# A transformer block on one core: the division of the attention output moves from VectorE to GpSimd, with a new order of steps

## The reference

```python
h = layernorm(x) * (1 + ca) + sa
q, k = [content, rotary] parts of 16 heads;  v from the 64-wide latent
attn = softmax(q @ k.T * SCALE + causal_mask)
out  = attn @ v                      # divided by the sums of the exponentials
x = x + ga * (out @ w_out.T)
h = layernorm(x) * (1 + cb) + sb
x = x + gb * mixture_of_8_experts(h) # gate, up, SiLU, weights of the top 8, down
```

## Time and profile before

| | us |
|---|---|
| median of three runs | 1096.62 |
| lowest, highest | 1093.07, 1107.65 |
| the profiled execution, timed | 1096.97 |
| its span in the profile | 1095.0 |
| busy: TensorE, VectorE, GpSimd, ScalarE | 1026.2, 771.5, 412.7, 401.1 |
| mean granted TensorE clock | 0.979 of full |

### The profile page before, as it was taken

One profiled execution on the slowest core, in us unless ns is written; L12 is line 12 of the kernel. 1 busy time (PEld: TensorE's weight loads), 2 busy tenths in 40 slices (PEclk: granted clock), 3 DMA queues, 4 the chain that ended last, 5 costly groups with the idle time before them and its releaser, 6 DMA issues.

```text
span 1095.0 us, 24777 instructions
## 1 busy us (share of the span) xinstructions
PE 1026.2 (94%) x9744; PEld 730.9 (67%) x9744; DVE 771.5 (70%) x1516; ACT 401.1 (37%) x723; POOL 412.7 (38%) x349
## 2 busy tenths in 40 slices
PE   6979989999999989999899999999999998999778
PEld 4646667766677667766677666776677666776456
DVE  5767687585957868677885859678686777857344
ACT  3334533254314443145332543144431453314310
POOL 1526442264505353154422644054441544226100
PEclk9989999999999999999999999999999999999979
DMA  6220000200002000200002000020002000010000
GB/s 191 58 88 2 2 1 1 68 2 2 1 4 67 2 1 1 69 2 2 1 1 69 2 2 1 2 69 2 1 1 69 2 2 1 1 49 2 1 1 20
DMA packets 22232, 23.59 MB, mean 22 GB/s; under 512 B 6314, under 2 KB 20138, under 8 KB 22130
## 3 DMA queue, kind: packets, MB, share of 16 engines
q1 hardware_dynamic: 22130, 22.02, 6.6%
HBM read 17.80 MB, written 4.21 MB: 20 GB/s over the span
## 4 chain that ended last, share of the span: by engine, by line
PE 82%; DVE 11%; issue 4%; ACT 2%; POOL 1%; DMA 1%; POOLq 0%; DVEq 0%; SPq 0%; ACTq 0%
PE ring L1131 17%; PE ring L981 12%; PE ring L982 10%; PE ring L983 10%; PE ring L1203 8%; PE av L1147 7%; PE ring L1107 6%; PE ring L1098 3%; DVE mcol L863 2%; DVE xr L902 1%; PE ring L1115 1%; PE ring L1192 1%; DVE prod L839 1%; PE av L1160 1%; PE ring L1042 1%
## 5 line engine op out<-in xcount | busy, mean ns | idle before, releaser
L672 ACT ACTIVATE pt<-ring 128x384 f32<-128x384 f32 (+1 forms) x384 | 170.9, 532 | 326.2 <-PE ring L1131 289.7
L562 POOL TENSOR_SCALAR_AFFINE_SELECT pt<-pt 128x512 f32<-128x512 f32 x128 | 79.4, 635 | 409.6 <-ACT pt L672 409.6
L863 DVE TENSOR_REDUCE mcol<-ring 128x1 f32<-128x128 f32 (+3 forms) x512 | 212.3, 483 | 19.3 <-PE ring L1107 18.1
L839 DVE TENSOR_TENSOR prod<-ring,table 128x1024 f32<-128x1024 f32 x128 | 155.4, 1219 | 93.1 <-PE ring L983 92.5
L1131 PE MATMUL ring<-rows 32*128 32x512 f32 (+3 forms) x3072 | 175.9, 330 | 9.4 <-ACT pt L672 4.9
L1131 PEld LDWEIGHTS ring<-rows 32*128 32x128 f32 x3072 | 130.4, 184 | 60.6 <-issue 35.0
L553 POOL TENSOR_TENSOR rows<-prod,rows 128x1024 fp32r<-128x1024 f32 x64 | 152.5, 2393 | 36.3 <-ACT rows L652 36.3
L546 POOL TENSOR_TENSOR prod<-prod 128x512 f32<-128x512 f32 x64 | 82.5, 1290 | 134.3 <-DVE prod L839 133.7
L652 ACT ACTIVATE rows<-prod 128x1024 fp32r<-128x1024 f32 x64 | 67.0, 1060 | 60.2 <-PE ring L1131 39.3
L1147 PE MATMUL av<-pt,vals 128*17 128x512 f32 (+3 forms) x1024 | 85.3, 439 | 3.2 <-POOL pt L562 3.2
L1131 PE MATMUL ring<-cont 32*128 32x512 f32 (+3 forms) x1024 | 85.6, 319 | 0.0
(11 more groups left out here) (162 smaller groups left out, 1624.4 us busy)
## 6 DMA issues: line engine op xcount, KB each, us to landing
xn<-x_dram SPq DMA_DIRECT2D x8, 512.0 KB, 4.1
xr<-x_dram SPq DMA_DIRECT2D x8, 512.0 KB, 4.2
out_dram<-xr SPq DMA_DIRECT2D x8, 512.0 KB, 3.2
gate_bc<-gates_scratch SPq DMA_DIRECT2D x8, 256.0 KB, 4.3
pt<-wmod_dram SPq DMA_DIRECT2D x1, 1536.0 KB, 6.6
pt<-gup_t_dram SPq DMA_DIRECT2D x16, 96.0 KB, 2.6
dn<-wu_t_dram SPq DMA_DIRECT2D x1, 640.0 KB, 10.1
xr<-wk_t_dram SPq DMA_DIRECT2D x1, 512.0 KB, 8.3
```

Of the source, the lines that this page charges most:

```text
L672: sc.activation(pt[:, PT_AT[n] + h * w:PT_AT[n] + (h + 1) * w], ps[:, 0:w], ACT.Exp, scale=SCALE).then_inc(exp_ready.sem, 1)
L839: ve.tensor_tensor(prod[:, s % PROD, :, :], ps[:, :].unsqueeze(1).broadcast_to([P, 2, S]), table[:, :, :], ALU.mult).then_inc(rotated.sem, 1)
L863: last = ve.reduce_max(mcol[:, q, h * HR + HD:h * HR + HD + 1], ps[:, at:at + (q + 1) * P], AX_X)
```

## The change

- A step `norm.0 g` on GpSimd does the multiplication of L883 by the inverted sums, the same tiles and shape. It waits for `sums_inverted` of its group, and for even g for `pair_ready` of the pair before, whose data its output overwrites.
- `attn_out` on VectorE keeps the wait for `normalised` of the group before, the turning of `av` and the reciprocal. Its wait for `pair_ready` goes.
- A step `pair.0 i` on VectorE waits for `normalised` of group 2i + 1 and turns the pair.
- BODY_ORDER and LAST_ORDER are new as a whole; SETUP_ORDER stays. The set of the other steps is the same in both.

Read by engine, the part of the new BODY_ORDER around the last group is: on TensorE score.032, rope.1010, qcon.10, value.031, value.032, latent.1, rope.1011, mix.00, mix.01, values.10, kcon.10, rope.1100, qcon.11, rope.1101, rope.1110, turn2.00, turn2.01, maxima.100, rope.1111, logits.0. On VectorE attn_out.02, rotate.1001, rotate.1010, pair.00, attn_out.03, qcon_lo.10, pair.01, latent_lo.1, rotate.1011, mixed, stats2.0, rotate.1100, norm2.0, kcon_lo.10, rotate.1101, qcon_lo.11, rotate.1110, low2. On GpSimd clear.030, combine.100, clear.031, norm.02, clear.032, norm.03, lo.100, combine.101, pow2.0.

```diff
 BODY_ORDER = """
-load_next.1 loads.0 maxima.010 rope.0200 reduce.010 score.000 rotate.0200 rope.0201 exp.000 rotate.0201 maxima.011
-rope.0210 clear.000 reduce.011 score.001 rope.0211 exp.001 rotate.0210 combine.020 clear.001 maxima.012 rotate.0211
-combine.021 value.000 value.001 reduce.012 score.002 hi.020 shift.01 qcon.02 lo.020 exp.002 kcon.02 qcon_hi.02
-clear.002 rope.0300 shifted.01 stats1.1 hi.021 qcon_lo.02 kcon_hi.02 score.010 rotate.0300 pow1.1 value.002 exp.010
-rope.0301 kcon_lo.02 score.011 attn_out.00 lo.021 rope.0310 rotate.0301 exp.011 maxima.020 clear.010 value.010
-rotate.0310 combine.030 reduce.020 score.012 exp.012 norm1.1 rope.0311 maxima.021 qcon.03 rotate.0311 reduce.021
-maxima.022 combine.031 clear.011 qcon_hi.03 kcon.03 hi.030 clear.012 qcon_lo.03 lo.030 hi.031 turn1.10 reduce.022
-value.011 turn1.11 kcon_hi.03 modulate1.10 shift.02 kcon_lo.03 shifted.02 lo.031 maxima.030 reduce.030 value.012
-modulate1.11 low1.10 score.020 exp.020 score.021 low1.11 clear.020 exp.021 attn_out.01 clear.021 rope.1000
-maxima.031 rotate.1000 value.020 reduce.031 maxima.032 reduce.032 value.021 score.022 exp.022 shift.03 shifted.03
-rope.1001 score.030 clear.022 value.022 rotate.1001 exp.030 attn_out.02 latent.1 latent_hi.1 latent_lo.1 combine.100
-score.031 clear.030 value.030 exp.031 score.032 clear.031 rope.1010 exp.032 clear.032 rope.1011 value.031 value.032
-hi.100 lo.100 rotate.1010 rotate.1011 kcon.10 kcon_hi.10 attn_out.03 values.10 rope.1100 combine.101 hi.101 mix.00
-mix.01 values.11 rotate.1100 kcon_lo.10 qcon.10 mixed.00 mixed.01 values_out.10 qcon_hi.10 lo.101 qcon_lo.10
-maxima.100 stats2.0 reduce.100 values_out.11 maxima.101 rope.1101 rope.1110 pow2.0 norm2.0 turn2.00 reduce.101
-turn2.01 rotate.1101 modulate2.00 rope.1111 modulate2.01 qcon.11 qcon_hi.11 rotate.1110 combine.110 low2.00
-maxima.102 low2.01 logits.0 rotate.1111 logits_copy.0 qcon_lo.11 gate.00 hi.110 combine.111 turn_l.0 lo.110
-reduce.102 turned_l.0 tanh.00 hi.111 gate.01 tanh.01 gate.02 tanh.02 gated.00 up.00 up.01 top.0 shift.10 gate.03
-gated.01 gated.02 up.02 ex.0 tanh.03 upped.00 top2.0 gate.04 turn_w.0 wT.0 gated.03 upped.01 up.03 gate.05
-shifted.10 wT_lo.0 upped.02 weigh.00 weigh.01 up.04 tanh.04 upped.03 gated.04 weigh.02 tanh.05 gated.05 weighed.00
-kcon.11 lo.111 up.05 weighed.01 upped.04 weighed.02 weigh.03 weigh.04 weigh.05 upped.05 weighed.03 weighed.04
-kcon_hi.11 weighed.05 down.00 kcon_lo.11 down.01 join.00 join.01 store.0
+load_next.1 loads.0 maxima.010 reduce.010 score.000 exp.000 rope.0200 rotate.0200 maxima.011 clear.000 reduce.011
+rope.0201 score.001 rope.0210 rotate.0201 exp.001 maxima.012 clear.001 rotate.0210 reduce.012 combine.020 value.000
+score.002 rope.0211 shift.01 kcon.02 rotate.0211 exp.002 qcon.02 hi.020 shifted.01 qcon_hi.02 value.001 clear.002
+value.002 combine.021 stats1.1 kcon_hi.02 score.010 hi.021 lo.020 kcon_lo.02 lo.021 rope.0300 qcon_lo.02 attn_out.00
+exp.010 maxima.020 rotate.0300 rope.0301 reduce.020 score.011 rope.0310 rotate.0301 exp.011 maxima.021 rotate.0310
+pow1.1 clear.010 reduce.021 norm.00 norm1.1 value.010 clear.011 score.012 combine.030 rope.0311 rotate.0311 exp.012
+combine.031 hi.030 maxima.022 kcon.03 qcon.03 clear.012 kcon_hi.03 reduce.022 turn1.10 qcon_hi.03 kcon_lo.03
+turn1.11 qcon_lo.03 value.011 hi.031 lo.030 modulate1.10 shift.02 shifted.02 maxima.030 reduce.030 modulate1.11
+value.012 low1.10 low1.11 score.020 exp.020 score.021 exp.021 clear.020 clear.021 attn_out.01 maxima.031 value.020
+reduce.031 norm.01 lo.031 maxima.032 value.021 reduce.032 score.022 exp.022 shift.03 rope.1000 shifted.03 score.030
+rotate.1000 clear.022 value.022 rope.1001 attn_out.02 exp.030 clear.030 rotate.1001 score.031 exp.031 combine.100
+clear.031 value.030 score.032 exp.032 rope.1010 qcon.10 qcon_hi.10 norm.02 clear.032 value.031 hi.100 value.032
+latent.1 rotate.1010 pair.00 attn_out.03 latent_hi.1 norm.03 lo.100 qcon_lo.10 rope.1011 pair.01 latent_lo.1 mix.00
+mix.01 values.10 kcon.10 rotate.1011 rope.1100 mixed.00 mixed.01 combine.101 qcon.11 values_out.10 rope.1101
+stats2.0 hi.101 kcon_hi.10 pow2.0 qcon_hi.11 rotate.1100 norm2.0 kcon_lo.10 rope.1110 turn2.00 turn2.01 rotate.1101
+modulate2.00 qcon_lo.11 modulate2.01 lo.101 maxima.100 rotate.1110 rope.1111 low2.00 combine.110 low2.01 logits.0
+gate.00 reduce.100 logits_copy.0 rotate.1111 maxima.101 tanh.00 turn_l.0 gate.01 gated.00 gate.02 reduce.101 gate.03
+gate.04 tanh.01 up.00 tanh.02 tanh.03 turned_l.0 gated.01 top.0 tanh.04 up.01 gated.02 gated.03 maxima.102 gated.04
+ex.0 up.02 top2.0 upped.00 hi.110 turn_w.0 upped.01 reduce.102 wT.0 gate.05 combine.111 tanh.05 up.03 up.04 wT_lo.0
+weigh.00 gated.05 weigh.01 upped.02 upped.03 up.05 weighed.00 weigh.02 weigh.03 upped.04 kcon.11 weighed.01 weigh.04
+upped.05 weighed.02 hi.111 weigh.05 kcon_hi.11 weighed.03 weighed.04 lo.110 weighed.05 down.00 shift.10 lo.111
+down.01 kcon_lo.11 shifted.10 values.11 join.00 values_out.11 join.01 store.0
 """
...
 LAST_ORDER = """
...
+score.030 clear.022 value.022 attn_out.02 exp.030 clear.030 score.031 exp.031 clear.031 value.030 score.032 exp.032
+norm.02 clear.032 value.031 value.032 pair.00 attn_out.03 norm.03 pair.01 mix.00 mix.01 mixed.00 mixed.01 stats2.0
...
@@ -537,6 +537,14 @@
                         i = int(kind[-1]) - 1
                         wait(pool, var_ready[i], b, ahead, 0)
                         pool.tensor_tensor(rstd, veps, half_neg[:, :], ALU.pow).then_inc(rstd_ready[i].sem, 1)
+                    elif kind == "norm":
+                        g = step[2]
+                        at = (g % 2) * HD
+                        wait(pool, sums_inverted, b, ahead, g)
+                        if g % 2 == 0:
+                            wait(pool, pair_ready, b, ahead, g // 2 - 1)
+                        pool.tensor_tensor(norm_out[:, :, at:at + HD], turned_out[:, :, 0:HD],
+                                           rsum.unsqueeze(2).broadcast_to([P, S // HR, HD]), ALU.mult).then_inc(normalised.sem, 1)
                     elif kind == "combine":
 
                         g, t = step[2:]
@@ -872,19 +880,14 @@
                     elif kind == "attn_out":
                         g = step[2]
                         wait_alone(ve, normalised, b, ahead, g - 1)
-                        if g % 2 == 0:
-                            wait_alone(ve, pair_ready, b, ahead, g // 2 - 1)
                         wait(ve, value_added, b, ahead, g * NST + NST - 1)
                         ve.transpose(room[:, 0, :], av[:, :]).then_inc(av_read.sem, 1)
                         wait(ve, av_read, b, ahead, g)
                         ve.reciprocal(rsum, turned_out[:, :, HD]).then_inc(sums_inverted.sem, 1)
-                        wait(ve, sums_inverted, b, ahead, g)
-                        at = (g % 2) * HD
-                        ve.tensor_tensor(norm_out[:, :, at:at + HD], turned_out[:, :, 0:HD],
-                                         rsum.unsqueeze(2).broadcast_to([P, S // HR, HD]), ALU.mult).then_inc(normalised.sem, 1)
-                        if g % 2:
-                            wait(ve, normalised, b, ahead, g)
-                            ve.transpose(on[:, g // 2, :], room[:, 1, :]).then_inc(pair_ready.sem, 1)
+                    elif kind == "pair":
+                        i = step[2]
+                        wait_alone(ve, normalised, b, ahead, 2 * i + 1)
+                        ve.transpose(on[:, i, :], room[:, 1, :]).then_inc(pair_ready.sem, 1)
                     elif kind == "mixed":
                         i = step[2]
                         if i == 0:
```

More of the change, by code:

```diff
@@ L105 @@
+ex.0 up.02 top2.0 upped.00 hi.110 turn_w.0 upped.01 reduce.102 wT.0 gate.05 combine.111 tanh.05 up.03 up.04 wT_lo.0
+weigh.00 gated.05 weigh.01 upped.02 upped.03 up.05 weighed.00 weigh.02 weigh.03 upped.04 kcon.11 weighed.01 weigh.04
+upped.05 weighed.02 hi.111 weigh.05 kcon_hi.11 weighed.03 weighed.04 lo.110 weighed.05 down.00 shift.10 lo.111
+down.01 kcon_lo.11 shifted.10 values.11 join.00 values_out.11 join.01 store.0
 """
 LAST_ORDER = """
-loads.0 maxima.010 rope.0200 reduce.010 score.000 rotate.0200 rope.0201 exp.000 rotate.0201 maxima.011 rope.0210
@@ L109 @@
-clear.000 reduce.011 score.001 rope.0211 exp.001 rotate.0210 combine.020 clear.001 maxima.012 rotate.0211
-combine.021 value.000 value.001 reduce.012 score.002 hi.020 shift.01 qcon.02 lo.020 exp.002 kcon.02 qcon_hi.02
-clear.002 rope.0300 shifted.01 hi.021 qcon_lo.02 kcon_hi.02 score.010 rotate.0300 value.002 exp.010 rope.0301
-kcon_lo.02 score.011 attn_out.00 lo.021 rope.0310 rotate.0301 exp.011 maxima.020 clear.010 value.010 rotate.0310
-combine.030 reduce.020 score.012 exp.012 rope.0311 maxima.021 qcon.03 rotate.0311 reduce.021 maxima.022 combine.031
@@ L114 @@
-clear.011 qcon_hi.03 kcon.03 hi.030 clear.012 qcon_lo.03 lo.030 hi.031 reduce.022 value.011 kcon_hi.03 shift.02
-kcon_lo.03 shifted.02 lo.031 maxima.030 reduce.030 value.012 score.020 exp.020 score.021 clear.020 exp.021
```

(24 more changed lines are left out.)

## The result

| | before | after |
|---|---|---|
| median, us | 1095.78 (4 executions) | 1111.30 (4) |
| lowest, highest | 1093.07, 1107.65 | 1109.77, 1112.18 |
| ratio, 95% interval | | 1.0119 [1.0062, 1.0175] |
| span of the profiled execution | 1095.0 | 1110.3 |
| mean granted TensorE clock | 0.979 | 0.971 |

The changed kernel is 1.2% slower: the time rises by 15.5 us where 10 were forecast. 1111.3 lies at the upper edge of the forecast's own range (1100 to 1112). One program's executions differ with the granted clock: beside the experiments the kernel before took 1091.7 us at a mean of 0.985 and up to 1107.6 at 0.964, and its two executions at 0.971, the changed kernel's level, took 1101.7 us.

What follows compares the result with a forecast made beforehand. TensorE, busy 1026.2 of 1095.0 us, was taken as the bound. Per body 2.1 - 1.1 + 0.25 = +1.25 us, seven times +8.8, plus 0.7 (batch 0) and 0.5 (last block): +10, giving 1106 us, range 1100 to 1112.

Steps and rivals of the forecast that it cites:

- What bounds the kernel: TensorE, busy 1026.2 of 1095.0 us; the change acts only through its few us of idle or slow running.
- Part 1: Division moved from VectorE to GpSimd as norm: 0.75 us each, between 0.65 and 1.29.
- Part 2: GpSimd's clear.032 queued behind norm.02, which waits for pair.00, so value.032 waits: loss of 2.1 us per body.
- Part 3: From value to turn2 and the banks behind it: loss falls from 3.5 to 2.4 us, gain 1.1 per body.
- idle left: about 0.5: TensorE before turn2: 10.1 us of cover from the start of mix against a chain of 10.5.
- The wait of maxima.100: Behind turn2, for banks that rotate.1101 and qcon_lo.11 free: 1.5 to 1.8 us.
- Part 4: Rest of the new order, such as score.000 at a body's start and maxima.031: together +0.25 us per body.
- The sum: Per body 2.1 - 1.1 + 0.25 = +1.25 us, seven times +8.8; with batch 0 and last block +10.
- The ends: Outside the loop's repeated terms: batch 0 +0.7 us, last block +0.5 us.
- Rival 1: The wait before value.032 brings a clock dip in every body, 1.2 to 1.4 us each: 1115 us, chance 0.2.
- Rival 2: VectorE keeps up behind norm2, so maxima.100 finds its banks: some 1093 us, or 1089, chance 0.2.

Runs made afterwards that it cites:

- Experiments 1 and 9: Two runs on the changed kernel: pair.00 put directly behind attn_out.02, 1091.4 us; norm.02 put behind clear.032 on GpSimd, 1106.5 us.
- Experiment 2: The changed kernel with lo.101 put ahead of pow2.0 on GpSimd: 1095.9 us, ratio 0.997 to the kernel before.
- both repairs: The changed kernel with pair.00 directly behind attn_out.02 and lo.101 ahead of pow2.0: 1080.6 us, ratio 0.979 to the kernel before.

## Why the prediction held, point by point

- **What bounds the kernel, held:** TensorE's busy time did not move (1026.2 to 1024.0), only its idle time and clock.
- **Part 1, price of the division, held:** 0.62 us for 0.75, under the lower bound of 0.65 (half of L546 of before). The Trainium skill (GPSIMD Engine Reference, section 3.1 Elementwise) has a ratio of 1.96, by which an estimate was 0.84; against VectorE's 0.426 the ratio measured is 1.46.
- **Part 2, the queue behind `norm.02`, held and shown:** 2.1 us forecast, 1.82 measured. Rotation, `pair.00`, `norm.02`, clear.032 run as written; the shorter division is 0.13 of the difference. Experiments 1 and 9 remove the wait in two ways.
- **Part 3, `value` to `turn2`, right in its net and wrong in its parts.** (Bodies of after without a dip against the mean of before.) Given back: qcon.10, rope.1100, rope.1101, maxima.101, logits.0 and gate.00 are 4.8 us shorter together, where I had 3.5; about 0.5 of it are the dips of before. Lost: 3.4 us, where I had 2.4. The step that failed is "idle left: about 0.5" before `turn2`: the step in front of it is 2.0 us longer, 1.80 of them idle. I took norm2 at its old 1.37 us and let GpSimd's queue end at pow2.0; lo.101 comes next in it, and its 2.38 us lie beside norm2 (2.07 us more). Experiment 2 shows it: with lo.101 moved away 0.64 us of idle are left, near what I wrote. In the same chain 0.8 us came back that I hadn't seen either: `mixed`'s first addition, held by lo.101 before, takes 0.82 us (L905 at 671.19) for 1.64. The same collision stood in the earlier trace rows: the 1.50 us of L883 end just behind the 1.29 us of L546. The wait of maxima.100 came out at 1.4, below my 1.5 to 1.8, and rope.1111 took none of the 0.2 I gave it. It does not depend on norm2's lateness, as the 1.19 us of experiment 2 show. Net gain 1.4 for 1.1.
- **Part 4, too small:** score.000 +0.6, maxima.031 +0.5, shift.02 -0.6, as argued; the step from values.11 to maxima.010 takes 0.7 more, which I had not counted, `down` 0.3 less and maxima.010 0.2 less. About +0.7 for +0.25.
- **The sum:** 1.8 - 1.4 + 0.7 = 1.1 us per body for 1.25, which is what the undipped bodies show (129.1 against 128.0). The ends were -0.4 (batch 0, its dip left out) and -0.8 (last block) for +0.7 and +0.5. So the steps alone account for 6.6 - 1.2 = 5.4 us of the 15.3 between the spans. This goes by the forecast's own baseline, the mean of before with its dips. Undipped against undipped a body costs 1.6 us more (129.1 against 127.5), and the dips of before come off the clock's share: then about 10 us are steps and 5 to 6 the clock. The executions at one clock say the same, 1112.0 against 1101.7 us at 0.971.
- **Rival 1, the dip of the clock, came in part, and gave the other 10 us:** 9.0 us behind `turn2` in five of seven bodies and 1.5 where one body's start (score.000 at 4.6 instead of 3.1 us) has one. The sum took bodies of after without any. This is the term whose absence hid behind an overestimate of the ends: priced at 1.2 a dip, the rival had the size wrong too, since three of the dips cost 2.6 to 2.9 and two 0.5.
- **Rival 2, VectorE keeps up behind norm2:** not there, L859 (qcon_lo.11), whose bank maxima.100 needs, still ends late. With both repairs the time (1080.6) is below even what this rival gave.

So the forecast was near for a sound reason (Part 2) and because errors offset each other, which is luck: 5 us too much in the steps and ends, 10 too little in the clock, and in Part 3 more given back and more lost than written. Why a body pays the deep dip or not stays open: the steps from score.001 to `turn2` take the same time within 0.05 us in the loop's bodies with and without it.

## What to carry to other kernels

When an operation moves to another engine, write down the queue there in order, with the wait of each entry: an entry that waits blocks every later one that was ready, and one token (`pair.00` here) can be worth more than the whole change. Then lay the two engines' operations beside each other in time before and after; here each order had one GpSimd subtraction over a VectorE operation on the path, at different places. And judge a moved operation with its order, since either half alone may be worse than the two.
